# Moving work across both ends of a sparse attention stage, and one residual add by one step

## The reference, cut to what matters

```python
k = max(int(S * SPARSITY), 1)                 # 25 of 256 keys
scores = jnp.einsum('bhqd,bhkd->bhqk', Q, K) * scale
thr = jax.lax.top_k(scores, k)[0][..., k - 1:k]
masked = jnp.where(scores >= thr, scores, -jnp.inf)
probs = jax.nn.softmax(masked, axis=-1)
attn = jnp.einsum('bhqk,bhkd->bhqd', probs, V)
...
mixed = gate * distilled + (1.0 - gate) * attn
return mixed @ Wo.T + bo
```

## Time and profile before

| | |
|---|---|
| median of 3 runs | 1118.98 us (1114.26 to 1119.06) |
| the profiled execution | 1111.8 us, its span 1110.0 us |
| busy over the span | TensorE 86%, VectorE 71%, ScalarE 51%, GpSimd 41% |
| mean granted TensorE clock | 0.819 |

### The profile page before, as it was taken

The page is one execution under the profiler, slowest core; times in us unless marked ns, Lnnn a source line. Parts: engine busy times, 40 slices in busy tenths (PEclk is TensorE's granted clock), DMA queues, the critical chain, the costliest instruction groups (busy, mean ns, idle before and its releaser), DMA issues.

```text
span 1110.0 us, 18262 instructions
## 1 busy us (share of the span) xinstructions
PE 951.4 (86%) x5092; PEld 723.8 (65%) x5092; DVE 789.5 (71%) x3096; ACT 571.4 (51%) x1309; POOL 459.8 (41%) x538
## 2 busy tenths in 40 slices
PE   5869979779798898875999785999899999997994
PEld 3538867567576776755995574885566666666963
DVE  5545687999999999995555853346688786864333
ACT  4326655445454544533763451677666766752631
POOL 2530028888757857845004435002522041032034
PEclk9979985555555555555999997999999999998998
DMA  9845613000150000012774313651100000005852
GB/s 306 290 143 148 207 40 134 11 12 15 29 75 8 13 1 6 13 57 91 209 214 139 86 32 94 179 160 34 32 9 1 1 20 2 1 20 151 245 160 61
DMA packets 63444, 95.66 MB, mean 86 GB/s; under 512 B 12128, under 2 KB 41968, under 8 KB 63216
## 3 DMA queue, kind: packets, MB, share of 16 engines
q1 hardware_dynamic: 46256, 71.94, 22.2%
q0 software_dynamic: 6144, 12.60, 3.8%
q10 hardware_dynamic: 10944, 9.97, 2.7%
HBM read 69.94 MB, written 30.83 MB: 91 GB/s over the span
## 4 chain that ended last, share of the span: by engine, by line
PE 43%; POOL 10%; issue 7%; ACT 4%; DVE 4%; another core or an unknown queue 3%; DMA 1%; POOLq 0%; ACTq 0%; SPq 0%; DVEq 0%
PE bank L764 9%; PE bank L403 6%; PE bank L748 5%; PE bank L416 4%; POOL vb L1732 4%; PE bank L360 3%; POOL hb L1738 3%; PE bank L738 3%; PE bank L372 2%; PE bank L732 2%; POOL yg L2066 2%; PE bank L543 1%; PE bank L391 1%; POOL xsc L2051 1%
## 5 line engine op out<-in xcount | busy, mean ns | idle before, releaser
L2066 POOL DMA_INDIRECT yg<-ys,posg x96 | 96.0, 1000 | 144.8 <-DMA ys<-ysb 55.5
L1707 DVE MAX8 vb<-sg 128x8 f32<-128x256 f32 x384 | 146.3, 431 | 0.0
L1732 POOL TENSOR_SCALAR vb<-sS,vb 128x256 f32<-128x256 f32 x126 | 115.2, 925 | 65.0 <-DVE vb L1707 61.6
L2051 POOL DMA_INDIRECT xsc<-xnS,posu x96 | 96.2, 1002 | 63.8 <-DVE posu L1481 35.9
L1117 ACT ACTIVATE hb<-sS,negm 128x256 f32<-128x256 f32 x128 | 58.0, 501 | 120.3 <-POOL negm L2082 119.9
L403 PE MATMUL bank<-xbT,ws 128*128 128x256 f32 x456 | 114.5, 388 | 0.0
L360 PE MATMUL bank<-xnT,ws 128*128 128x512 f32 x192 | 99.2, 646 | 13.6 <-issue 8.7
L543 PEld LDWEIGHTS bank<-kn,qn 128*128 128x128 f32 x512 | 107.0, 308 | 0.0
L1709 DVE MATCH_REPLACE8 sg<-vb,sg 128x256 f32<-128x256 f32 x256 | 104.9, 426 | 0.0
L543 PE MATMUL bank<-kn,qn 128*128 128x17 f32 x512 | 101.4, 338 | 0.0
L372 PEld LDWEIGHTS bank<-ws,hb 128*128 128x128 f32 x512 | 67.2, 206 | 49.7 <-issue 38.1
(11 more groups left out here) (226 smaller groups left out, 1913.3 us busy)
## 6 DMA issues: line engine op xcount, KB each, us to landing
ws<-tab_m SPq DMA_DIRECT2D x46, 450.0 KB, 3.7
ws<-tab_m SPq DMA_DIRECT2D x54, 321.0 KB, 3.4
xb<-xsc SPq DMA_DIRECT2D x76, 128.0 KB, 2.7
ys<-ysb ACTq DMA_DIRECT2D x76, 128.0 KB, 3.4
xsc<-qn SPq DMA_DIRECT2D x3, 2048.0 KB, 10.7
pk<-packed SPq DMA_DIRECT2D x1, 3209.0 KB, 10.4
tab_m<-packed SPq DMA_DIRECT2D x5, 512.0 KB
ws<-packed SPq DMA_DIRECT2D x8, 256.0 KB, 4.6
```

What stands on the lines that cost most here:

```text
L1707: e.max(m8s[:, m:m + 8], s).then_inc(A["tk"], 1)
L1732: i = e.tensor_scalar(msk[:, n * S:n * S + S], sS[:, s:s + S], m[:, n, TOPK - 1:TOPK], None, ALU.is_ge)
L2051: e.indirect_dma_start(xsc[:, :], at(posu[g.p], t, k), xnS[:, g.tile(t)], None).then_inc(s_sc, 16)
L2066: e.indirect_dma_start(yg[:, y:y + D], None, ys[:, :], at(posg[g.p], t, k)).then_inc(s_g[t % GY], 16)
```

## The change

At the start of the attention: scores of 3 steps instead of 4 are made singly beside the blocks, the fourth step's pair of scores is made right behind block 17's products; the whole search of steps 0 to 2 stands beside the blocks (42 operations, 5 per block in blocks 7 to 10, 3 later, instead of 3 per block and 36 in all); ScalarE loads its exponential table before block 16's turn ends and makes the exponentials of steps 0 and 1 beside the last blocks; batch 1's statistics stand two blocks earlier. GpSimd issues two gathers in steps 1 and 2 and then one a step up to step 22, and VectorE combines a token tile one step later.

Inside: `dve_a0_x` stands at r = 6 instead of 7 in each batch; the gate's product and its ScalarE part stand one step earlier. At the end: part 2 of S1 is normalised, routed and placed one step earlier, its last scatters are spread by pairs, and the product of step 62 stands before the transposes of step 63.

```diff
-        LEAD, S_FIRST, SEARCH = 4, 5, 3
-        SEARCHED = SEARCH * (NBLK - S_FIRST - 2)
+        LEAD, S_FIRST = 3, 5
...
+        def searched(n):
+
+            k = n - S_FIRST - 2
+            return min(5 * max(min(k, 4), 0) + 3 * max(k - 4, 0), LEAD * TK)
...
+            elif n == NBLK - 2:
+
+                e.wait_ge(M["sg"], NBLK)
+                pe_a0_S(e, LEAD)
...
-        NORM_A0 = {23: 0, 39: 1, 55: 2}
+        NORM_A0 = {23: 0, 39: 1, 54: 2}
...
-        SCATTER_A0 |= {59 + n: 16 + n for n in range(5)}
+        SCATTER_A0 |= {58: (16, 17), 59: (17, 19), 60: (19, 20), 61: (20, 22), 62: (22, 23)}
...
-                    elif r == 6:
+                    elif r == 5:
                         pe_a0_gp(e, b + 1)
+            pe_a0_PV(e, 8 * B - 2)
             pe_a0_PT(e, 8 * B - 1)
-            pe_a0_PV(e, 8 * B - 2)
             pe_a0_PV(e, 8 * B - 1)
...
+            elif n == NBLK - 3:
+
+                e.preload_act_table_set("exp_and_others")
+            elif n == NBLK - 2:
+                act_a0_e(e, 0)
+            elif n == NBLK - 1:
+                act_a0_c(e, LEAD)
+                act_a0_e(e, 1)
...
-            e.preload_act_table_set("exp_and_others")
             act_a0(e)
...
-        COMBINE_A0 = {4 + 2 * t: t for t in range(GT)}
+        COMBINE_A0 = {5 + 2 * t: t for t in range(GT)}
...
-                if b > 0 and r == 7:
+                if b > 0 and r == 6:
                     dve_a0_x(e, b - 1)
...
-                if 1 <= a <= 2 * GT:
-                    pool_gather(e, S0, a - 1, a)
+                if a == 0:
+                    pool_a0_rstd(e, 1)
+                elif a <= 2:
+
+                    pool_gather(e, S0, 2 * a - 2, 2 * a)
+                elif a <= 2 * GT - 2:
+                    pool_gather(e, S0, a + 1, a + 2)
```

More of the change, by code:

```diff
@@ L590, in pe_beside_s0 @@
                 pe_a0_gp(e, 0)
-        NORM_A0 = {23: 0, 39: 1, 55: 2}
[L595 to L602, removed]
-        SCATTER_A0 |= {59 + n: 16 + n for n in range(5)}
+            elif n == NBLK - 2:
+                e.wait_ge(M["sg"], NBLK)
+                pe_a0_S(e, LEAD)
+        NORM_A0 = {23: 0, 39: 1, 54: 2}
+        T_A0 = {24: 0, 40: 1, 55: 2}
+        LOGITS_A0 = {25: 0, 41: 1, 56: 2}
+        TOP_A0 = {26: 0, 42: 1, 56: 2}
+        CHOICE_A0 = {27: 0, 43: 1, 56: 2}
+        RANK_A0 = {32: 0, 48: 1, 57: 2}
+        SCATTER_A0 = {33 + n: (n, n + 1) for n in range(8)}
+        SCATTER_A0 |= {49 + n: (8 + n, 9 + n) for n in range(8)}
+        SCATTER_A0 |= {58: (16, 17), 59: (17, 19), 60: (19, 20), 61: (20, 22), 62: (22, 23)}
+        SCATTERED_A0 = 23
         def pe_a0(e):
@@ L607, in pe_a0 @@
                 b, r = a // 8, a % 8
-                if LEAD <= a + 3 < 8 * B:
+                if LEAD < a + 3 < 8 * B:
                     pe_a0_S(e, a + 3)
@@ L1151, in act_a0 @@
                 b, r = a // 8, a % 8
-                act_a0_e(e, a)
-                if LEAD <= a + 3 < 8 * B:
+                if a >= 2:
+                    act_a0_e(e, a)
+                if LEAD < a + 3 < 8 * B:
                     act_a0_c(e, a + 3)
@@ L1169, in act_a0 @@
                         act_a0_Ve(e, b + 1)
-                    elif r == 7:
+                    elif r == 6:
                         act_a0_gate(e, b + 1)
@@ L1743, in dve_beside_s0 @@
                 dve_late(e)
[L1744 to L1748, removed]
+            for i in range(searched(n), searched(n + 1)):
+                dve_a0_topk(e, i // TK, i % TK, i % TK + 1)
+            if n == NBLK - 3:
                 dve_a0_norm(e, 1)
-        COMBINE_A0 = {4 + 2 * t: t for t in range(GT)}
+        COMBINE_A0 = {5 + 2 * t: t for t in range(GT)}
         def dve_a0(e):
@@ L1768, in dve_a0 @@
                     dve_a0_norm(e, b + 1)
-                dve_a0_topk(e, a, min(max(SEARCHED - TK * a, 0), TK))
+                if a >= LEAD:
+                    dve_a0_topk(e, a)
                 if a in COMBINE_A0:
@@ L2086, in pool_a0 @@
                 b, r = a // 8, a % 8
-                if b + 1 < B and r == 0:
+                if b > 0 and b + 1 < B and r == 0:
                     pool_a0_rstd(e, b + 1)
@@ L2093, in pool_a0 @@
                     any_select(e, a)
-                if 1 <= a <= 2 * GT:
-                    pool_gather(e, S0, a - 1, a)
+                if a == 0:
[4 more added lines that the diff above has]
+                    pool_gather(e, S0, a + 1, a + 2)
                 if a in SCATTER_A0:
-                    pool_scatter(e, S1, SCATTER_A0[a], SCATTER_A0[a] + 1)
+                    pool_scatter(e, S1, *SCATTER_A0[a])
         def pool_a1_rstd(e, c):
@@ L2145, in gpsimd_program @@
             pool_a0(e)
-            pool_scatter(e, S1, len(SCATTER_A0))
+            pool_scatter(e, S1, SCATTERED_A0)
             pool_rstd(e, D1.m)
```

## The result

The changed kernel takes 1128.68 us (median of 4 runs, 1128.42 to 1130.04), the kernel before 1118.62 beside it; ratio 1.0095, 95% interval 1.0074 to 1.0117. I had forecast 1124.0 in a range of 1113 to 1132. The time lies in the range, but "slower by more than 0.5%" had only 0.40, less than "no change", and my own case of +2 to +8 us was passed too.

The account below looks back on a forecast made before the run. The prediction took VectorE to bound the attention and TensorE S0's blocks. Start -10.3, middle +16.5 and end -1.1 sum to +5.1 us, which on the median of 1118.98 gives 1124, range 1113 to 1132.

Parts of the forecast that it names:

- my own case: The prediction's own forecast for the whole kernel: slower by +2 to +8 us, chance 0.42.
- start: Start of the attention: gaps -6.4, search -2.0, blocks' last result -2.9, new waits +1.0; -10.3 us (-7.8 to -11.3).
- middle: Batches 1 to 7: VectorE's earlier add waits for TensorE's last product of the batch before, +16.5 us (12 to 19).
- end: End of the attention: earlier last scatter spares S1's first block its 1.08 us row wait; -1.1 us (0 to -1.5).
- The gaps and the search beside the blocks: Start: both VectorE gaps before combines close, -6.4 us; six searches leave the attention, -2.0, costing nothing beside the blocks.
- Then GpSimd's 4.7 us is less than VectorE's 4.97 plus half a combine: After the start's waits: GpSimd's step with a gather is shorter than VectorE's search plus half a combine; no separate size.
- The waits for scores: Start: VectorE waits for scores, 0.5 us at step 5, 0.3 to 0.5 at step 6; +1.0, at most 3.5.
- The middle's other batches: VectorE's waits at the earlier add, batches 2 to 7: 1.7, 0.5, 3.9, 2.8, 3.9, 2.0 us.
- The waits halve: Rival: waits at the add halve while the start's gain stands; change about 0, 1119 us; chance 0.20.
- TensorE's clock: Clock case, which the forecast range leaves out; the prediction as given states no size or chance.
- The reordered products gain about what the later transposes lose: End of the attention: the new order of last products and transposes about cancels out; part of the end's -1.1 us.
- the late GpSimd: Rival at the start: gathers stay late, VectorE waits at steps 5 and 6, -6.4 shrinks to -2; +9.5, 1128.5 us; chance 0.18.

Follow-up runs that it names:

- e5: The changed kernel with the add to x at r = 7 and part 2's tables, scatters and last products as before; 1109.78 us, ratio 0.9936.
- e6: The changed kernel with the transposes of step 63 again ahead of the products of step 62; 1125.29 us, ratio 1.0078.
- e3: The changed kernel with one gather in each of steps 1 to 24 instead of two in steps 1 and 2; 1125.80 us, ratio 1.0070.
- e2: The kernel before with one edit, the add to x at r = 6 instead of 7; 1135.32 us, ratio 1.0171.
- e8: The changed kernel with one gather in each of steps 2 to 25; 1124.86 us, ratio 1.0072.
- e4: The changed kernel with a batch's last product at the end of r = 4 and its mixing earlier in ScalarE's list; 1117.81 us, ratio 0.9997.
- e9: The kernel of e5 with step 11's combine moved behind the eighth operation of step 12's search; 1114.51 us, ratio 0.9942.
- e1: The changed kernel with the add to x back at r = 7 in every batch but batch 6; 1116.26 us, ratio 0.9991.

## Why the prediction was right in sign and short in size

The sum was +5.1 and the stretch shows +10.27. Term by term: start -10.3 forecast, -7.6 measured (e5); middle +16.5, 18.6 measured; end -1.1, by difference -0.8 (the 1.08 us that S1's first block no longer waits for its rows, less what the reorder costs, e6). Some 0.3 us of the +10.27 are the clock in S1's first block, 0.73 against 0.76.

**The gaps and the search beside the blocks: right.** Both combines find their rows. Six more operations of the search cost the blocks nothing; VectorE's last `ysb` of S0 stands at 157.87, less the 1.92 us of late start 155.95, where I said 155.6. Step 9's search starts 10.7 us earlier, reckoned the same way, 0.7 of it since one combine fewer stands ahead of it.

**"Then GpSimd's 4.7 us is less than VectorE's 4.97 plus half a combine": true, and the step that failed.** I used it to say that nothing is left over from the start. But GpSimd comes into the attention with a backlog, and 4.97 + 0.35 - 4.64 = 0.7 us a step is all it can make up. In the kernel before, the two gaps of VectorE did that work: they were 6.4 us in which GpSimd caught up, to the point of waiting 2.32 us itself. With the gaps closed and two more gathers ahead it is 8.9 us behind at step 9, where it was 3.4. Of these 5.5 us more, 3.2 go with the two gathers (e3 has 5.7); the other 2.3 I put down to the closed gaps, by difference, since no run kept the gaps under the new gathers. The waits for scores that I had feared at steps 5 and 6 (+1.0) didn't come, only one of 0.44 at step 3, whose scores I had costed at nothing. The backlog was paid at the next places where VectorE meets a result from behind GpSimd: batch 1's norm, 1.2 us, and batch 1's add, 5.04 where I had 1.7. That is 3.3 of the missing microseconds, plus 1.2. e2 (the old start: 2.35 at the add), e3 and e8 (fewer gathers first: 3.25 and 2.32) show it from both sides.

**The held combines: missed.** 1.4 us, which no row of the kernel before showed at that size; its longest there is 0.47.

**The middle's other batches: right, each within half a microsecond (batch 3 just so).** Forecast 1.7, 0.5, 3.9, 2.8, 3.9, 2.0 for batches 2 to 7; measured 1.63, 0, 3.83, 2.76, 3.84, 1.54. The prediction's way of getting them, laying the start of a search beside the end of the product, is right to 0.1 us where TensorE's list has no gap. e2 reproduces it and e4 moves it by 2.6 us with a product's place. Batch 7's was an estimate along another path, through GpSimd's scatters and ScalarE, and no run changed the scatters alone: e2, with the old ones, has no wait there, and e4 can't move it, so it fits. (In its terms three times 0.91 is 2.7 and not 2.9, which changes little.) "The waits halve" and "TensorE's clock" both fall: the changed kernel's granted clock is 0.50 and 0.52 in the two windows above, at or near the lower level, and TensorE needs the same 20.8 us for its stretch as before.

**"The reordered products gain about what the later transposes lose": wrong by 0.45 us** (e6).

**The chances.** Since the start could only come out smaller and batch 1's wait only larger if GpSimd was late, both errors had the same cause; I had taken them as separate, and the late GpSimd (0.18) as something that would show as waits for scores at steps 5 and 6. That rival's time, 1128.5, is almost the measured one, and that is luck: it let the gaps' gain shrink to 2 us, whereas the gaps closed whole and the late GpSimd was paid for at batch 1. It had the engine right and the place wrong. My chance of "slower" was also added short: 0.18, 0.08 and two fifths of 0.42 make 0.43, not 0.40.

## What to carry to other kernels

A gap on the engine that bounds a stage is often where a second engine catches up. Before you count a closed gap as gain, look at who trails whom by how much on both sides of it, and ask where that distance is paid next. An operation that consumes another engine's last product has a distance that can be read off two timelines to a tenth of a microsecond; moving it ahead by one step costs the step less that distance, in every repetition. And where whole times scatter, measure between two landmarks around the change, and put both where the clock is the same in all kernels: here half a microsecond was readable up to the last norm, while S1's first block behind it differed by up to 1.4 us that no edit had made.

## What the runs showed of the hardware that I had not expected

A gather can take nearly three times as long beside a big load. The second gap of the earlier trace rows isn't a late gather: in e3 the fourth gather is issued at 177.47 and its combine goes only at 184.67, 7.2 us later, while the first pair before the change needed 174.44 - 171.85 = 2.6 us. In between lies the load of `pk`, 3209 KB, issued at 175.44 in SyncE's queue. Timelines of GpSimd and VectorE, and busy time by stretch, in e3:

```profile
177.47 1.05 POOL L2082 DMA_INDIRECT yg<-ys,posg  x1 [0.15 <-POOL hb L1755]
...
184.67 0.35 DVE L1616 SCALAR_TENSOR_TENSOR x<-yg,pw,x 128x128 f32<-128x128 f32 x1 [0.96 <-DMA yg<-ys,posg]
```

```profile
176.00:184.00 8.00, 8.00 (x37) 6.63 (x35) 7.71 (x31) 3.98 (x13) 7.49 (x9) 0.50 0.96 375
184.00:192.00 8.00, 8.00 (x36) 6.39 (x35) 7.19 (x30) 4.37 (x13) 7.49 (x9) 0.50 0.16 63
```

The DMA engines are busy 0.96 of the first stretch and 0.16 of the next. The load ends at about the time at which the row lands. That the load holds the gather up is read from the coincidence, in the kernel before and in e3 alike. e8 supports it: there the fourth gather is issued at 178.46, 6.3 us behind the load (172.16) instead of 2.0, and its combine goes 4.35 us later instead of 7.2. No run left the load out. The changed kernel escapes it because its first four gathers are out by 172.4.

And a VectorE operation on two tiles can take 1.33 us instead of 0.35 beside GpSimd's product (e9). The columns of busy time don't show it, since the hold counts as VectorE's work.

The granted clock makes a part of a trace incomparable that the edits don't touch: the same eight products of S1's first block take 3.62 us in e5 and 2.65 in e1. What makes it rise sooner in e1, no run here shows.
